# One stretch of a two-layer post-norm kernel on one core: the work between the rank and the gate in a new order on four engines

## The reference

```python
x = _layernorm(x + _L0_attn_ref(...))   # linear attention over a 256 x 256 Gram matrix
x = _layernorm(x + _L0_ffn_ref(...))    # gate: softmax over 8 experts, threshold 0.1, weighted sum of 8 products
x = _layernorm(x + _L1_attn_ref(...))   # qkv, 16 heads, softmax over the 16 heads of each token, projection
x = _layernorm(x + _L1_ffn_ref(...))    # router score; the top 768 of 1024 rows go through gelu(row @ w_block)
# in the last one: _, top_idx = top_k(scores, k); out = x.at[batch_idx, top_idx].set(processed)
```

## Time and profile before

| | us |
|---|---|
| median of 3 runs | 1390.96 |
| lowest, highest | 1388.37, 1396.16 |
| the profiled execution | 1388.98 |
| its span, first to last instruction | 1387.0 |
| TensorE busy (matmuls) | 1175.5 |
| VectorE busy | 925.7 |
| ScalarE busy | 732.5 |
| GpSimd busy | 578.7 |

### The profile page before, as it was taken

How to read it: one execution, slowest core, us unless ns; L and a number is a source line. 1 busy time by engine, 2 the same in 40 slices (tenths; PEclk the granted TensorE clock), 3 DMA queues, 4 the chain that set the end, 5 groups by cost and what they waited for, 6 DMA issues and landing times.

```text
span 1387.0 us, 31167 instructions
## 1 busy us (share of the span) xinstructions
PE 1175.5 (85%) x12264; PEld 751.8 (54%) x12264; DVE 925.7 (67%) x2113; ACT 732.5 (53%) x1156; POOL 578.7 (42%) x887
## 2 busy tenths in 40 slices
PE   6688898998989899998989899998989888775643
PEld 3444456655655556655665556655665546542542
DVE  3544677587766878587776877577766877465624
ACT  3222475346654685347653685347654685355623
POOL 3135335425535545425525535425525525333212
PEclk8689998899979998899979997899969998798566
DMA  5000091205611191206611191205610091207220
GB/s 183 15 1 16 31 158 13 78 14 128 88 32 47 47 173 13 77 16 137 78 32 47 47 173 11 78 10 126 94 31 33 31 172 13 62 1 188 26 62 31
DMA packets 93145, 90.64 MB, mean 65 GB/s; under 512 B 7110, under 2 KB 81864, under 8 KB 92744
## 3 DMA queue, kind: packets, MB, share of 16 engines
q1 hardware_dynamic: 79560, 75.02, 28.3%
q0 software_dynamic: 2560, 8.39, 1.7%
q10 hardware_dynamic: 10880, 5.25, 1.5%
HBM read 46.68 MB, written 41.94 MB: 64 GB/s over the span
## 4 chain that ended last, share of the span: by engine, by line
PE 40%; DVE 20%; POOL 12%; ACT 9%; issue 8%; DMA 7%; SPq 2%; ACTq 1%; POOLq 0%; DVEq 0%
PE bank L1573 37%; POOL stage L585 4%; DMA ct<-scratch_qkv 3%; DVE keys L1355 3%; SPq L458 2%; POOL rs L535 2%; DVE x L1260 2%; DVE stats L1119 2%; DVE gelu L1357 2%; DMA bt<-scratch_o 2%; ACT shared L698 2%; DVE ct L1089 1%; DMA scratch_o<-stage 1%; PE bank L1583 1%; ACT x L821 1%
## 5 line engine op out<-in xcount | busy, mean ns | idle before, releaser
L1573 PE MATMUL bank<-we,at 128*128 128x512 f16 x1536 | 370.6, 400 | 1.9 <-DVE x L1260 1.9
L1573 PEld LDWEIGHTS bank<-we,at 128*128 128x128 f16 x1536 | 153.8, 102 | 192.1 <-issue 37.6
L550 POOL TENSOR_TENSOR part<-part 128x512 f32<-128x512 f32 x64 | 84.1, 1313 | 279.9 <-ACTq L847 279.9
L698 ACT ACTIVATE part<-bank,wexp 128x256 f32<-128x256 f32 x256 | 104.8, 473 | 160.9 <-PE bank L1573 103.0
L1573 PE MATMUL bank<-bt,wqkv 128*128 128x512 f16 x576 | 138.9, 383 | 23.4 <-DVE stage L1089 17.0
L821 ACT ACTIVATE x<-x,nm,rs 128x256 f32<-128x256 f32 x192 | 105.1, 596 | 100.0 <-POOL nm L538 98.7
L1260 DVE SCALAR_TENSOR_TENSOR x<-bank,wexp,x 128x256 f32<-128x256 f32 x256 | 122.8, 480 | 49.8 <-PE bank L1573 43.2
L531 POOL TENSOR_SCALAR nm<-mv 128x2 f32<-128x2 f32 x128 | 34.9, 272 | 253.8 <-DVE mv L1124 248.3
L1089 DVE TENSOR_TENSOR stage<-bank,stage 128x512 f16<-128x512 f32 x112 | 75.6, 686 | 89.1 <-ACT stage L698 88.9
L1573 PE MATMUL bank<-keys,blockdiag 128*128 128x16 f16 x3072 | 97.0, 193 | 20.1 <-DVE blockdiag L1287 9.7
L698 ACT ACTIVATE stage<-bank 128x512 f16<-128x512 f32 x112 | 66.1, 597 | 82.7 <-PE bank L1573 77.0
(11 more groups left out here) (181 smaller groups left out, 2253.8 us busy)
## 6 DMA issues: line engine op xcount, KB each, us to landing
scratch_qkv<-stage SPq DMA_DIRECT2D x40, 512.0 KB, 3.3
ct<-scratch_qkv SPq DMA_DIRECT2D x120, 128.0 KB, 6.8
x_in<-in_x_dram SPq DMA_DIRECT2D x32, 256.0 KB, 2.7
keys<-scratch_qkv SPq DMA_DIRECT2D x64, 128.0 KB, 5.8
bt<-scratch_o SPq DMA_DIRECT2D x16, 512.0 KB, 3.8
out_dram<-x POOLq DMA_DIRECT2D x32, 256.0 KB, 2.6
scratch_qkv<-part SPq DMA_DIRECT2D x8, 512.0 KB, 8.4
scratch_o<-stage SPq DMA_DIRECT2D x32, 128.0 KB, 3.4
```

The source lines that it names most:

```text
L550: pool.tensor_tensor(part[:, 0:2, :], part[:, 0:2, :], part[:, 2:4, :], ALU.add)\
L698: return act.activation(dst, src, ACT.Copy, scale=scale)
L1573: ins = pe.matmul(dst, lhs, rhs, start=(n == 0), stop=(n == len(terms) - 1))
```

## The change

No operation is added or removed and none is changed; the calls of turn stand in another order on VectorE, ScalarE, GpSimd and TensorE. SyncE keeps its order. VectorE's a_cb is cut in two, so that its second instruction can stand later:

```diff
@@ vector engine
             def a_cb(a):
                 dve.wait_ge(a_full, a_filled(a, "CB"))
                 dve.tensor_tensor(c32[:, :], a_ps("CB")[:, 0:D], gt[:, :], ALU.mult).then_inc(a_free[a_ring("CB")], 1)
+
+            def a_cb_lo(a):
                 dve.wait_ge(c_hi, a + 1)
                 split_lo(c16[32:33, :], c32[32:33, :], rowtmp[32:33, 0:D]).then_inc(c_lo, 1)
...
                     a_cb(a)
                 if b is not None:
+                    a_ln2(b, 3)
+                if a is not None:
+                    a_cb_lo(a)
+                if b is not None:
                     b_tx(b, 0)
...
+                if a is not None:
+                    a_tx(a, 3)
+                if b is not None:
+                    b_tx(b, 1)
                 if c is not None:
                     b_ff(c, 0)
-                if b is not None:
-                    a_ln2(b, 3)
-                if a is not None:
-                    a_tx(a, 3)
+                if a is not None:
+                    a_ap(a, 0)
+                if b is not None:
+                    b_tx(b, 2)
+                    b_tx(b, 3)
+                    b_f(b, 0)
                 if c is not None:
                     b_ff(c, 1)
...
@@ gpsimd
+                if b is not None:
+                    ln(b, 7, 0)
                 if c is not None:
                     ln(c, 4, 1)
...
@@ scalar engine
+                if b is not None:
+                    b_tx(b, 1)
+                    a_ln2n(b, 3)
                 if c is not None:
                     b_res(c, 1)
+                if b is not None:
+                    b_tx(b, 2)
+                    b_tx(b, 3)
+                if c is not None:
                     b_ff(c, 1)
                 if b is not None:
-                    b_tx(b, 1)
-                if c is not None:
+                    b_f(b, 0)
+                if c is not None:
+                    b_ffn(c, 0)
                     b_res(c, 2)
                     b_res(c, 3)
...
@@ tensor engine
                 if c is not None:
                     b_ff(c, 2)
-                    b_ff(c, 3)
-                if a is not None:
-                    a_ap(a, 1)
                 if b is not None:
                     b_tx(b, 3)
                     b_f(b, 0)
+                if c is not None:
+                    b_ff(c, 3)
+                if a is not None:
+                    a_ap(a, 1)
...
                 if b is not None:
-                    b_f(b, 10)
+                    b_f(b, 11)
                 if a is not None:
                     a_gate(a)
-                if b is not None:
-                    b_f(b, 11)
-                if a is not None:
-                    a_moe(a, 0, (0,))
+                    a_moe(a, 0, (0, 1))
                     a_wt(a)
-                    a_moe(a, 0, (1, 2))
+                    a_moe(a, 0, (2,))
```

More of the change, by code:

```diff
@@ L1048, in turn @@
                 if a is not None:
+                    to_at_hi(a, "TY1", 1, 5)
+                if c is not None:
+                    b_ffn(c, 2)
+                if b is not None:
+                    b_f(b, 7)
+                if a is not None:
                     a_apn(a, 2)
                 if b is not None:
-                    b_f(b, 7)
                     if b == NB - 1:
@@ L1054, in turn @@
                     b_f(b, 8)
+                if c is not None:
+                    b_ffn(c, 3)
+                if b is not None:
+                    b_f(b, 9)
                 if a is not None:
@@ L1489, in turn @@
                 if b is not None:
+                    a_ln2(b, 3)
+                if a is not None:
+                    a_cb_lo(a)
+                if b is not None:
                     b_tx(b, 0)
-                if b is None and c is not None:
-                    for p in range(TP):
-                        b_ff(c, p)
-                    return
+                if a is not None:
+                    a_tx(a, 3)
+                if b is not None:
+                    b_tx(b, 1)
                 if c is not None:
                     b_ff(c, 0)
-                if b is not None:
-                    a_ln2(b, 3)
-                if a is not None:
-                    a_tx(a, 3)
-                if c is not None:
-                    b_ff(c, 1)
-                if b is not None:
-                    b_tx(b, 1)
                 if a is not None:
@@ L1508, in turn @@
                     b_tx(b, 2)
+                    b_tx(b, 3)
+                    b_f(b, 0)
+                if c is not None:
+                    b_ff(c, 1)
                 if a is not None:
@@ L1527, in turn @@
                     b_f(b, 5)
+                if c is not None:
+                    b_ff(c, 3)
+                if b is not None:
+                    b_f(b, 6)
                 if a is not None:
```

74 lines of the change are left out of this document (25 added, 49 removed).

## The result

The changed kernel takes 1463.82 us (median of 4 runs, 1458.09 to 1465.77) against 1392.56 of the kernel before on the same chip: a ratio of 1.0506, with a 95% interval of 1.0463 to 1.0549. That is 5% slower. The direction was forecast; the size was not, and the time lies above the range. The profiled execution took 1458.09 us, with a span of 1456.2 against 1387.0.

What follows compares the result with a forecast made beforehand. TensorE was taken to pace rank to gate, with 6.05 us of waits a turn. Profiled 1388.98, plus 36.6 for loops less tail, 7.8 for the clock, less 0.8 for other turns, gave 1432.6 us; range 1403 to 1456.

Steps and rivals of the forecast that it cites:

- Head: Before the QKV projection: earlier fourth layer norm removes a 1.51 us wait; first feed at 627.5 instead of 630.49.
- apn 0: ScalarE's first normalise of a over x2: no gain, at 634.9 against 635.01 before.
- Loops: ScalarE's four normalises of a wait in series for store, landing and copy: 7.5, 8.8, 6.5 us; gate 7.4 later.
- The section on both ways of the landing: Output stores landing in 3.36 us, not the median 2.6: up to 2.1 us a turn more, kept for the range.
- Sum of the loops: From the first to the fourth normalise of a on ScalarE: 22.8 us against 15.37 before.
- Tail: From gate to next turn's first matmul: 1.3 us less, 10.4, with the gate's softmax costed at nothing.
- Clock: TensorE's clock falls after waiting ahead of the fourth transposition: 1.3 us a turn, 7.8 in all, bounds 0 and 3.0.
- Other turns: Turn 8 gains 1.5 us and turn 1 loses 0.7: together -0.8, bounds -4 and +3.
- Rival 1: The projection, not the stores, paces the order, so TensorE keeps the gain: 13.4 us off, 1375.6; chance 0.10.
- Rival 2: Later stretches absorb the loss, as next turn's loads come relatively earlier: 1395 us or less; chance 0.08.
- Rival 3: Worse store landings and a longer slow clock: 66.4 us more, 1455.4; chance 0.14.

Runs made afterwards that it cites:

- c1: e4 plus earlier evictions of x2, ahead of feed-forward additions, and two order swaps on GpSimd: 1396.5 us.
- e2: The changed kernel, but SyncE issues q's loads later, behind the last of the projection's stores before the gate: 1444.6 us.
- e4: The kernel before with only the earlier fourth layer norm and the later gate, without the changed loops: 1379.7 us.
- e6: The kernel before with only the gate moved behind the last projection and the experts' first two passes ahead of the gate's transposed weights: 1387.6 us.
- after: The changed kernel itself, with the whole change against the kernel before: 1463.8 us, ratio 1.0506.
- e3: The changed kernel with unused products filling TensorE's waits, 16 ahead of the third transposition of x1 and 12 ahead of the fourth: 1462.3 us.
- the good order: The order of e4, to which single groups of the changed kernel's moves were added: 1379.7 us.
- e1: The changed kernel with c's normalised rows stored from idle tiles, so GpSimd's copies wait for the normalise, not the landing: 1429.1 us.

## Why the prediction failed, point by point

- **Head.** F0 was put 13.03 us after the rank (627.5 less 614.47) and came at 651.69 - 638.66 = 13.03. Right; but c1 shows that evictions moved ahead of the additions, as here, make the copies late.
- **apn 0.** Forecast 20.4 after the rank, measured 659.02 - 638.66 = 20.36. Right: the head's gain does not get through.
- **Loops: the step that failed.** apn 0 to apn 1 was to be 7.5 and is 7.62; apn 2 to apn 3 was to be 6.5 and is 6.60. apn 1 to apn 2 was to be 8.8 and is 11.34 in turn 4 and 13.0 to 13.5 in the others. The steps were right, and only the 2.65 us for store 2's landing was mis-sized. In this loop the sum had the landing run under the two layer norms that GpSimd does between store 2 and copy 2 (4.2 us with the store itself), so it cost nothing; with 6.5 to 8.7 us it comes out from under them by 2.5 to 4.7. Where it lands in 2.6 to 3.2 (e2), the loop is 8.8. The section on both ways of the landing looked at the row of 3.36 us, but kept 0.7 us for each of the three passes without slack; the price was 2.5 to 4.7 on one pass, and on the one that had slack. The premise that failed is unsaid there: that the loads of q still come behind the store. SyncE's order did not change, so the loads kept their time (28.6 us after the rank, before 29.9), while the store moved from 26.3 to 31.9. By the steps' own times this could have been seen.
- **Sum of the loops.** apn 0 to apn 3 takes 27.2 us on average (25.6 to 27.8) in place of the 22.8: 4.4 x 6 = 26 us, against 25.5 between the forecast of 1432.6 and the profiled 1458.1.
- **Tail.** Forecast 10.4; it is 11.0 at full clock (e4, e6) and 12.2 to 12.7 where the clock is 0.76 to 0.79. Costing the gate's softmax at nothing was wrong by 0.6, of the 1.3 that were to show without its cover: two banks did not cover it. In turn 4 of after TensorE waits behind them for the softmax's result:

```profile
693.52 0.30 PE L1689 MATMUL bank<-const,gsel 128*128 128x128 f32 x1 [0.26 <-DVE gsel L1227]
```

- **Clock.** It fell as forecast (0.89 to 0.93, and 0.76 to 0.99 behind the gate), after waits of 3.75 us in turn 4 and 5.94 in turn 5 ahead of ty 2 and of 2.90 and 2.68 ahead of ty 3, where one of 4.0 ahead of ty 3 was forecast. The term of 1.3 us a turn is there at its place: apn 3 to the gate takes 4.5 us in place of 3.24 in five turns of six. It is not there in the whole, since e3 got the clock back and gained nothing: a stretch's loss by the clock can't be added to the time as it stands.
- **Other turns.** -0.8 was forecast; gate 7 to rank 8 takes 110.6 (before 110.7), and nothing came.
- **Not in the sum.** The stretch from next turn to rank is 1.9 us shorter a turn, with a granted clock of 0.92 to 0.89 against 0.89 to 0.87. With the tail's miss of up to 2.3 this about cancels. That one term explains the rest so closely is therefore in part luck.
- **Rivals.** Rival 1 (paced by the projection) falls with the three waits for ScalarE. Rival 2 (absorbed) got 9.3 us back, not the loss. Rival 3 (1455.4) named worse landings, the right mechanism, and was the nearest. Its nearness is in part luck: it spread 2.1 us a turn over three passes where one pass took 2.5 to 4.7, and its 3.0 us for the clock made up for a part of what that left out.

## What to carry to other kernels

Where a buffer is handed on by a landing, price that landing by what is in flight when the moved transfer starts, and lay the new issue times of the other queues beside it, of those too whose order did not change. A group of steps that runs ahead of its consumer is worth its slack: the three passes moved, with GpSimd's order beside them, put the whole loop in series, and no other part that was tried on the good order came near it (1.0 and 2.4 us a turn against 13.3). Undo parts in both directions and compare by stretch; taken back one at a time from the slow side, the first three parts here moved the gate by less than 2 us together.

## What the runs showed of the hardware

- **A store waits behind another engine's loads, and its data with it.** Store 2 of turn 4 (GpSimd, issued at 670.57) lands 6.5 us later, at 677.09. The two loads of q that SyncE issued at 669.54 and 670.03 land 6.84 and 7.53 us later, at 676.37 and 677.56: the store arrives between them, so ahead of one that was issued 0.5 us before it. In the other five full turns it lands behind every load issued ahead of it. In e1 it lands behind a load that was issued 0.3 us after it, in all six. So landings go nearly, not strictly, by the order of issue. The issues of three windows of 0.1 us, each with its size and its time to landing:

```profile
ct<-scratch_qkv SPq DMA_DIRECT2D x1, 128.0 KB, 6.8
...
ct<-scratch_qkv SPq DMA_DIRECT2D x1, 128.0 KB, 7.5
...
out_dram<-x POOLq DMA_DIRECT2D x1, 256.0 KB, 6.5
```

  The trace has the packets of each queue as well. q0 is that of the output stores (2560 packets in all, 80 for each of 32), q1 has SyncE's transfers. From the store's issue to 673.80, and from there to 676.50, with packets, MB and their time as a share of 16 engines:

```profile
q1 hardware_dynamic: 744, 0.36, 124.2%
...
q1 hardware_dynamic: 606, 0.29, 64.6%
q0 software_dynamic: 80, 0.26, 44.2%
```

  In the first 3.2 us none of the store's packets moved, while q1's took all of the transfer engines' time; the first packet came 3.4 us after the issue, in the other full turns 5.5 to 6.0, where it is 1.4 for the other stores of turn 4. From the last packet to the landing it is 0.7 us, against 0.4 for those stores. In e2, with no load of q ahead of it, store 2's first packet comes after 1.4 us in every full turn. So it was the data that was late. The estimate of 2.6 us, by fixed part and size, that the prediction took from the Trainium skill ("Anatomy of one DMA") agrees with the median of 2.7 and not with this store; the measurement decides. The Trainium skill has another section that bears on it (DMA: Bandwidth & Descriptors, "Queues, rings and completion order"): the semaphore increment of a transfer lands only after every earlier write of the same transfer engine, across its queues. That rule can account for no more than the 0.3 to 0.4 us that the landing lags further behind the last packet than usual, and not for the rest. Why q0's packets had to wait for q1's, no run here shows.
- **A load moved out of the way is not free.** Eight loads right behind eight others land in 9.7 to 11.6 us in place of 4.1 to 8.3, and the next stage pays.
- **Clock.** A whole turn with its three stretches at 0.89, 0.79 and 0.92 and one at 1.00, 1.00 and 0.89 took 167.22 and 167.74 us (turn 3 of after and of e3).
